# Attention with two wide fp32 parts instead of three bf16 parts, heads stacked in partition halves, and value matmuls carried into the next step

## The reference

```python
x = x + attn(layernorm(x))
# attn: 16 heads of 16 columns, each batch 1024 positions
q, k, v = x @ Wq, x @ Wk, x @ Wv
k_eff1 = w[0] * k1 + w[1] * k2          # w = softmax(quadrant_weights)
k_eff2 = w[2] * k1 + w[3] * k2
attn = softmax((q1 @ k_eff1.T + q2 @ k_eff2.T) * scale)
out = (attn @ v) @ Wo
```

## Time and profile before

| | us |
|---|---|
| median of 3 runs (2004.94 to 2010.0) | 2007.19 |
| the profiled execution | 2008.85 |
| its span | 2007.1 |

### The profile page before, as it was taken

The page is one execution under the profiler, slowest core; times in us unless marked ns, Lnnn a source line. Parts: engine busy times, 40 slices in busy tenths (PEclk is TensorE's granted clock), DMA queues, the critical chain, the costliest instruction groups (busy, mean ns, idle before and its releaser), DMA issues. The chain is left out here.

```text
span 2007.1 us, 38130 instructions
## 1 busy us (share of the span) xinstructions
PE 1746.5 (87%) x10689; PEld 1076.5 (54%) x10690; DVE 1293.4 (64%) x2730; ACT 1016.1 (51%) x2046; POOL 458.4 (23%) x597
## 2 busy tenths in 40 slices
PE   6949999999999999998869986999978549999990
PEld 5802333233233233222758875989876249988880
DVE  7759888788788788871458868555546662222224
ACT  4614777667677677777235432344322225554442
POOL 4636000000000000000101224322122155555550
PEclk9957999999999999999879997999988759999995
DMA  4562221122221122200010001131311922222117
GB/s 152 162 149 32 33 33 33 35 33 33 35 33 33 35 33 33 33 1 1 0 12 1 0 11 44 44 84 42 85 43 51 339 91 66 65 65 65 63 63 259
DMA packets 119479, 121.80 MB, mean 61 GB/s; under 512 B 20692, under 2 KB 97512, under 8 KB 119208
## 3 DMA queue, kind: packets, MB, share of 16 engines
q1 hardware_dynamic: 106568, 94.35, 19.9%
q0 software_dynamic: 7584, 20.72, 3.2%
q10 hardware_dynamic: 5184, 4.98, 0.7%
HBM read 88.04 MB, written 31.59 MB: 60 GB/s over the span
## 5 line engine op out<-in xcount | busy, mean ns | idle before, releaser
L1873 DVE TENSOR_REDUCE mx<-ps 128x1 f32<-128x512 f32 x1024 | 634.9, 682 | 104.5 <-PE ps L2020 104.2
L1947 ACT ACTIVATE PR<-ps 128x512 f32<-128x512 f32 x1024 | 533.9, 607 | 189.5 <-PE ps L2081 186.1
L2020 PE MATMUL ps<-KQ 96*128 96x512 bf16 x1024 | 408.7, 405 | 34.2 <-PEq L210 25.3
L2081 PE MATMUL ps<-KQ 99*128 99x512 bf16 x1024 | 391.8, 389 | 18.5 <-issue 9.8
L2020 PEld LDWEIGHTS ps<-KQ 96*128 96x128 bf16 x1024 | 99.5, 99 | 360.0 <-DVE mx L1873 270.1
L2046 PE MATMUL ps<-PR,VO 128*32 128x512 f32 x2048 | 270.3, 606 | 0.0
L2081 PEld LDWEIGHTS ps<-KQ 99*128 99x128 bf16 x1024 | 99.7, 98 | 143.7 <-ACT PR L1947 59.2
L1968 POOL COPY VO<-V 128x512 f32 (+1 forms) x16 | 9.8, 615 | 719.8 <-PE ps L2046 719.6
L1746 PEld LDWEIGHTS ps<-e_xinT,e_w 128*128 128x128 f32 x1264 | 156.6, 195 | 5.8 <-issue 1.9
L1746 PE MATMUL ps<-e_xinT,e_w 128*128 128x128 f32 x1264 | 157.5, 279 | 1.1 <-ACT e_xinT L1678 1.1
L1736 PE MATMUL ps<-eW,e_hiddenT 128*128 x632 | 154.9, 388 | 3.1 <-issue 1.1
(11 more groups left out here) (289 smaller groups left out, 2354.0 us busy)
## 6 DMA issues: line engine op xcount, KB each, us to landing
KQ<-qk_parts SPq DMA_DIRECT2D x192, 128.0 KB, 4.7
TB<-toeplitz_lines SPq DMA_DIRECT2D x32, 512.0 KB, 5.9
qk_parts<-parts SPq DMA_DIRECT2D x8, 1536.0 KB, 6.8
eW<-in_L_ffn_W SPq DMA_DIRECT2D x16, 512.0 KB, 6.3
eW<-in_L_ffn_W SPq DMA_DIRECT2D x8, 1024.0 KB, 12.0
e_got<-expert_outputs SPq DMA_DIRECT2D x16, 512.0 KB, 9.7
X<-in_L_attn_x SPq DMA_DIRECT2D x8, 512.0 KB, 4.7
expert_inputs<-e_xn SPq DMA_DIRECT2D x8, 512.0 KB, 3.2
```

The source lines that it names most:

```text
L1873: nc.vector.reduce_max(mx[:, k, h, q:q + 1], ps[:, bank(r, ("max", t))], AX).then_inc(red_done, 1)
L1947: nc.scalar.activation(PR[:, kt % 2, h, qc * BANK:(qc + 1) * BANK], ps[:, st_bank(r, s)], ACT.Exp).then_inc(exp_done, 1)
L2020: nc.tensor.matmul(ps[:, bank(r, ("max", t))], KQ[r][0:KROWS, 1, h, q * P:(q + 1) * P], KQ[r][0:KROWS, 0, h, k * BANK:(k + 1) * BANK], sta ...
L2081: nc.tensor.matmul(ps[:, st_bank(r, s)], KQ[r][0:AROWS, 0, h, kt * P:(kt + 1) * P], KQ[r][0:AROWS, 1, h, qc * BANK:(qc + 1) * BANK], start ...
```

## The change

The two sides `q` and `k` are split into two fp32 parts (the kind that TensorE multiplies in one pass, `F32R`) instead of three bf16 ones, and three pairs of parts are stacked instead of six: 48 rows, 50 with the maxima's two parts. Two heads of a unit lie in partitions 0 to 63, two in 64 to 127 (`HALF`, `HR`). The third split and its copy on ScalarE and GpSimd go; parts are stored as fp32. `load_qk` issues 12 DMAs as before, each for two heads; the rows of maxima take four DMAs instead of three.

The first pass writes the two halves of a row of scores to two neighbouring banks (two pairs of banks in place of three single ones), and one reduction over 1024 elements replaces two over 512 and gives the maximum already negated. `negate` has two operations. `EARLY` still says 12 and `LATE` 4, now counted in rounds of two matmuls.

The blocks go through all key tiles for the first half of the queries, then for the second: 16 steps of four blocks (one per head), one value group per step, into a single bank. A step's value group is issued after the second block of the next step, and the last one of a unit in the first step of the next unit. The output is copied by ScalarE in two halves of 512 (`keep_heads`), in the second step of the next half. `VO` has three buffers. After every block comes one maxima matmul of the next units.

```diff
-PARTS = 3
-PAIR_Q = [0, 0, 1, 0, 2, 1]
-PAIR_K = [0, 1, 0, 2, 0, 1]
+PARTS = 2
+PAIR_Q = [0, 1, 0]
+PAIR_K = [0, 0, 1]
 KROWS = len(PAIR_Q) * HD
 AROWS = KROWS + PARTS
+HALF = P // 2
+HR = HG // 2
...
-                KQ = [sbuf(st, f"KQ{r}", [P, 2, HG, SEQ], BF16) for r in range(2)]
+                KQ = [sbuf(st, f"KQ{r}", [P, 2, HR, SEQ], F32R) for r in range(2)]
...
                     for side, pairs in ((1, PAIR_Q), (0, PAIR_K)):
                         for j, part in enumerate(pairs):
-                            src = pqk.rearrange("s a k p t -> s a (k p) t").rearrange("s a (g h c) t -> s a g c h t", h=HG, c=HD)
-                            sp.dma_start(KQ[r][j * HD:(j + 1) * HD, side],
-                                         src[1 - side, part, ds(g, 1), :, :, ds(SEQ * b, SEQ)].rearrange("g c h t -> (g c) h t")).then_inc(kq_loaded[r], 16)
+                            for y in range(2):
+                                row = HALF * y + HD * j
+                                sp.dma_start(KQ[r][row:row + HD, side].bitcast(F32),
+                                             src[1 - side, part, ds(g, 1), :, HR * y:HR * (y + 1), ds(SEQ * b, SEQ)].rearrange("g c h t -> (g c) h t")).then_inc(kq_loaded[r], 16)
...
-                                for m in range(2 * DK):
-                                    pool.wait_ge(mid_ready, 2 * DK * c + m + 1)
-                                    nc.gpsimd.tensor_tensor(part(h, m, 2), rest[:, m], part(h, m, 1), op=ALU.subtract).then_inc(lo_ready, 1)
...
-                                    dve.wait_ge(lo_ready, 2 * DK * c + m + 1)
-                                    nc.vector.tensor_tensor(rest[:, m], ps[:, 2 + m], part(h, m, 0), op=ALU.subtract).then_inc(rest_ready, 1)
+                                    nc.vector.tensor_tensor(part(h, m, 1), ps[:, 2 + m], part(h, m, 0).bitcast(F32), op=ALU.subtract).then_inc(lo_ready, 1)
...
-                                for m in range(2 * DK):
-                                    act.wait_ge(rest_ready, 2 * DK * c + m + 1)
-                                    nc.scalar.copy(part(h, m, 1), rest[:, m]).then_inc(mid_ready, 1)
...
-    VO = sbuf(stack, "VO", [P, KT, HG, 2 * HD])
...
+    VO = sbuf(stack, "VO", [P, RING, KT, HG, 2 * HD])
...
-    SLOTS = 3
-    MAX_BANK, ST_BANK, OT_BANK = 0, SLOTS, 2 * SLOTS
+    SLOTS, PAIRS = 3, 2
+    MAX_BANK, ST_BANK, OT_BANK = 0, 2 * PAIRS, 2 * PAIRS + SLOTS
...
-    BLOCKS, MAXES, NM = KT * HG * QC, HG * QT * QC, 5
-    order = [(h, q, k) for h in range(HG) for q in range(QT) for k in range(QC)]
-    LOADS = 2 * len(PAIR_Q)
+    STEPS = QC * KT
+    BLOCKS, MAXES, NM = STEPS * HG, HG * QT, 2
+    ROWS = 2 * PARTS
+    order = [(HR * y + x, q) for q in range(QT) for x in range(HR) for y in (1, 0)]
+    LOADS = 4 * len(PAIR_Q)
     EARLY = 12
-    TURN = EARLY + 8
-    LATE = 5
+    TURN = EARLY + 5
+    LATE = 4
...
+            nc.vector.memset(nmp[:], 0.0).then_inc(ready, 1)
...
-                nc.vector.reduce_max(mx[:, k, h, q:q + 1], ps[:, bank(r, ("max", t))], AX).then_inc(red_done, 1)
-            def negate(u):
+                nc.vector.tensor_reduce(mx[:, r, h * QT + q:h * QT + q + 1], ps[:, b:b + 2].rearrange("p a n -> p (a n)"), AX, ALU.max, negate=True).then_inc(red_done, 1)
...
+            def keep_heads(u, qc):
+                act.wait_ge(pv_done, STEPS * u + KT * (qc + 1))
+                if not is0(u):
+                    act.wait_ge(ot_tr, u)
+                nc.scalar.copy(OT[:, qc * BANK:(qc + 1) * BANK], ps[:, OT_BANK]).then_inc(ot_kept, 1)
...
                 for s in range(BLOCKS):
-                    kt, h, qc = s // (HG * QC), s // QC % HG, s % QC
+                    step, h = s // HG, s % HG
+                    kt = step % KT
                     act.wait_ge(st_done, BLOCKS * u + s + 1)
-                    if h == 0 and qc == 0 and not (is0(u) and kt < 2):
-                        act.wait_ge(pv_done, KT * u + kt - 1)
-                    nc.scalar.activation(PR[:, kt % 2, h, qc * BANK:(qc + 1) * BANK], ps[:, st_bank(r, s)], ACT.Exp).then_inc(exp_done, 1)
-                    if nxt is not None and s == (BLOCKS - 8 if at(2) is not None else BLOCKS - 1):
-                        keep_rows(nxt[0], (nxt[2] + 1) % RING)
-                act.wait_ge(pv_done, KT * u + KT)
-                if not is0(u):
-                    act.wait_ge(ot_tr, 2 * u)
-                nc.scalar.copy(OT[:], ps[:, OT_BANK:OT_BANK + 2].rearrange("p a n -> p (a n)")).then_inc(ot_kept, 1)
+                    if h == 0 and not (is0(u) and step < 2):
+                        act.wait_ge(pv_done, STEPS * u + step - 1)
+                    nc.scalar.activation(PR[:, kt % 2, h], ps[:, st_bank(r, s)], ACT.Exp).then_inc(exp_done, 1)
+                    if kt == 1 and h == 0:
+                        if step > KT:
+                            keep_heads(u, 0)
+                        elif not is0(u):
+                            keep_heads(u - 1, 1)
+                    if nxt is not None and s == QC * (MAXES - EARLY + LATE) - 2:
+                        keep_rows(nxt[0])
             unit_loop(act, unit)
+            keep_heads(UNITS - 1, 1)
...
-            def weigh(u, kt, qc):
-                if qc == 0:
-                    pe.wait_ge(exp_done, BLOCKS * u + HG * QC * (kt + 1))
-                if kt == 0 and qc == 0:
+            def weigh(u, r, step):
+                kt = step % KT
+                pe.wait_ge(exp_done, BLOCKS * u + HG * (step + 1))
+                if step == 0:
                     pe.wait_ge(vo_ready, u + 1)
-                    if not is0(u):
-                        pe.wait_ge(ot_kept, u)
+                if kt == 0 and not (is0(u) and step == 0):
+                    pe.wait_ge(ot_kept, 2 * u + step // KT)
                 for h in range(HG):
-                    last = nc.tensor.matmul(ps[2 * HD * h:2 * HD * (h + 1), OT_BANK + qc], VO[:, kt, h], PR[:, kt % 2, h, qc * BANK:(qc + 1) * BANK],
+                    last = nc.tensor.matmul(ps[2 * HD * h:2 * HD * (h + 1), OT_BANK], VO[:, r, kt, h], PR[:, kt % 2, h],
                                             start=(kt == 0), stop=(kt == KT - 1))
-                if qc == QC - 1:
-                    last.then_inc(pv_done, 1)
+                last.then_inc(pv_done, 1)
...
                 for s in range(BLOCKS):
-                    kt, h, qc = s // (HG * QC), s // QC % HG, s % QC
+                    step, h = s // HG, s % HG
+                    kt, qc = step % KT, step // KT
                     if not (is0(u) and s < SLOTS):
                         pe.wait_ge(exp_done, BLOCKS * u + s - SLOTS + 1)
-                    nc.tensor.matmul(ps[:, st_bank(r, s)], KQ[r][0:AROWS, 0, h, kt * P:(kt + 1) * P],
-                                     KQ[r][0:AROWS, 1, h, qc * BANK:(qc + 1) * BANK], start=True, stop=True).then_inc(st_done, 1)
-                    if kt > 0 and h in (1, 3) and qc == 1:
-                        weigh(u, kt - 1, h // 2)
-                    while done < (s + 1) * len(beside) // BLOCKS:
-                        what, given = beside[done]
-                        what(*given)
-                        done += 1
-                for qc in range(QC):
-                    weigh(u, KT - 1, qc)
+                    nc.tensor.matmul(ps[:, st_bank(r, s)], KQ[r][half(h, AROWS), 0, h % HR, kt * P:(kt + 1) * P],
+                                     KQ[r][half(h, AROWS), 1, h % HR, qc * BANK:(qc + 1) * BANK], start=True, stop=True).then_inc(st_done, 1)
+                    t, k = divmod(s, QC)
+                    if t + EARLY < MAXES:
+                        if nxt is not None:
+                            first_pass(*nxt, t + EARLY, k)
+                    else:
+                        if after is not None:
+                            first_pass(*after, t + EARLY - MAXES, k)
+                    if s == QC * (TURN - EARLY) - 1 and not is0(u):
+                        turn_heads(u - 1)
+                    if s == QC * (MAXES - EARLY + LATE) - 1 and nxt is not None:
+                        turn_max(nxt[0])
+                    if h == HR - 1:
+                        if step > 0:
+                            weigh(u, r, step - 1)
+                        elif not is0(u):
+                            weigh(u - 1, (r + RING - 1) % RING, STEPS - 1)
```

More of the change, by code:

```diff
@@ L1906, in _ @@
                 reduce(0, 0, t)
-            negate(0)
+            negate(0, 0)
             for t in range(EARLY):
@@ L1986, in unit @@
                 (u, n, r), nxt, after = at(0), at(1), at(2)
-                sp.wait_ge(row_loaded[r], 16 * PARTS * (n + 1))
-                if after is not None and not is0(u):
+                sp.wait_ge(row_loaded[r], 16 * ROWS * (n + 1))
+                if is0(u):
+                    sp.wait_ge(ones_ready, 2)
+                elif after is not None:
                     sp.wait_ge(st_done, BLOCKS * u)
@@ L2023, in turn_max, with first_pass @@
-            def turn_max(u, r):
```

(24 more changed lines are left out.)

140 lines of the change are left out of this document (56 added, 84 removed).

## The result

The changed kernel takes 2029.8 us (median, 2024.8 to 2040.7) against 2007.9 of the kernel before on the same chip: 1.011 times as long, 95% interval 1.0088 to 1.0131. It is slower, clear of the noise, where 1972.5 was forecast, and the time lies outside the range of 1948 to 2008. The profiled execution has a span of 2030.4 us against 2007.1: +23.3, where the sum said -36.1.

A forecast was written before the change was run, and what follows sets the result against it. TensorE was taken as the bound. Stage start -1, before the loop +6.1, unit 0 -5, 14 units at -2.9 each and last unit +4.4 sum to -36.1: 2008.85 to 1972.8, kept as 1972.5 us; range 1948 to 2008.

The forecast's parts named there:

- The halves work at once, a pair costs 0.22: Loop: block and maxima matmul on different partition halves overlap, 0.22 us a pair; 0.44 if they don't.
- The rival "turns": Loop: the halves don't overlap, step 2.85 to 2.93 us, total 2036 to 2053, middle 2043; chance 0.14.
- Value group 1.00, ScalarE 0.49 per exponential, VectorE not the bound, idle 0.6 and 0.3 a step: Loop: operation times in us; VectorE needs 38.9 a unit, below 41.1; ScalarE idles 0.6, VectorE 0.3 per step.
- Step 2.57: Loop: chain of exponential, value group, block 3, its exponential 0.43 later, and exponential 4 makes a step 2.57 us.
- The partial rival: Loop: serial weight loads or a dearer value group, step 2.67, unit 47.1 or 47.2, about 1993 us; chance 0.14.
- Extras 4.4: Each loop unit: output copies 1.96, output transposes and wait 1.5, transposed maxima 0.9, together 4.4 us beyond 16 steps.
- Last unit +4.4: Last unit, without maxima: step from 2.40 to 2.57 (+2.7), two copies +2.0, boundary -0.3: 4.4 us longer.
- The rival "the clock": Loop: clock at half for a third of it, step at least 3.9 us, +120, about 2090; chance 0.03.
- Before the loop +6.1: Before the first block: 12 early rounds of full 1024, the last waiting for ten reductions; first block 6.1 us later.
- Unit 0 -5, stage start -1, rest 0: First unit 5 us shorter at 44; projection with loads and stores 1 us shorter; remaining program unchanged.

The follow-up runs named there:

- the two experiments on them: Changed kernel with last-unit dummy matmuls and copies moved before the third exponential: 1985.8 us; changed kernel with value group after the fourth block: 1986.6 us.
- The experiment: Changed kernel plus an unread matmul of the maxima's shape after each block left without a maxima matmul, mainly in the last unit: 2015.9 us.
- the pair of executions above: Changed kernel with value group after the fourth block, without and with the last unit's dummy matmuls: 1986.6 and 1977.5 us.

## Why the prediction was wrong, point by point

- *The halves work at once, a pair costs 0.22*: right. Pairs start together, and 0.24 from the next when TensorE runs on. The rival "turns" was built and gave the step it named, 2.83 for 2.85.
- *Value group 1.00, ScalarE 0.49 per exponential, VectorE not the bound, idle 0.6 and 0.3 a step*: right, within 0.02.
- *Step 2.57*: the term that failed is the 0.43 from a block to its exponential. It was read in the last unit of before, on a bf16 block, whose weight load of 0.10 stands behind the group too; the fp32 load there takes 0.18, and the way to the exponential 0.53. The row that says so was on the table: 195 against 99 ns in the earlier trace rows. I had used it for TensorE's sum, where it is hidden behind other matmuls, and not on the chain, where nothing hides it. 16 x 0.10 x 14 units = 22 us. The partial rival named this size, 2.67 and a unit of 47.1, for another reason.
- *Extras 4.4*: measured 4.8, of which the copies are 1.9 as counted. The copies' mechanism and size were right, and of the two experiments on them one took 1.3 of a unit away and the other 1.9; the rest of the extras was not measured term by term.
- *Last unit +4.4*: the main failure. I had weighed the clock for the loop alone, and for the last unit taken from the earlier trace rows that it stays at 1.00. But that row is of matmuls with 99 rows. In the changed kernel the loop has both halves at work and the last unit only one, and its granted clock is 0.61 in the mean from the last mark on. The experiment puts this at 22.7 us in that stretch, 24.7 in the span, 14 by the medians. The rival "the clock" had half clock at the wrong place, in the loop, at a chance of 0.03; and its argument, the share of time at work, doesn't tell the loop (2.0 of 2.67 us, 0.98) from the last unit (1.97 of 2.67, 0.61).
- *Before the loop +6.1*: measured +13.9. Three terms were too small: a reduction at half clock takes 1.27 and not 1.18 (44 of them, 4.0); three places where two rounds share a pair of banks (3 x 1.15 = 3.4), which the sum didn't have; and 2.4 instead of 2.0 for the memsets. They make the difference, 7.8. Where unit 0's bank pairs go by turns, two of the three places are gone and the first block comes 3.1 earlier than with 8 early rounds alone.
- *Unit 0 -5, stage start -1, rest 0*: the start gave 2.8 more and the rest 1.7 more. Of the +32.3 by which the first and last unit together missed, 22.7 is the clock and 1.6 the step of the last unit; the other 8 are not taken apart. Unit 0 is at half clock for its first 9.7 us (to 192.0), before for 3.5; at the 6.2 us that 19.8 us at half clock cost in the pair of executions above, that is an estimated 2. Of the loop's 24, a unit of 47.5 instead of 45.6 makes 14 x 1.9 = 27, 22 of it the step; the units at the turn of the hardware loop, which the sum did not look at, give some of it back.
- *Three sums*: the unit's terms add up to 45.5, not 45.6. In the partial rival, loads at 0.19 make a step of 8 x 0.19 + 1.09 = 2.61 and a unit of 46.2, not 47.2. And 1.06 and 1.2 over two slots are 1.13 a reduction, not 1.18, further from the measured 1.27. None changes which terms failed.

In one sentence: the change did what the forecast said it does in the loop, at 16.7 of the 40.6 us of gain, and the gain that was left was smaller than what the ends lost.

## What to carry to other kernels

Take the latency of a link in a chain from a row with the same type, and look at whether its weight load can hide: behind a value group or a wait it starts with its matmul in every row shown here. When a change halves the rows that a matmul uses, ask in every stretch, the last one too, whether the other half still has work, since the granted clock may follow it, as it did here in the last unit; a few matmuls that do nothing can then be cheaper than idle rows. Before moving the work itself, move who waits for a buffer: two blocks later was worth 2 us a unit.

## What the runs showed of the hardware that I had not expected

- With the two row halves by turns the mean granted clock of 14 units was 0.89, TensorE busy for 736 of 785 us; with both at once 0.98, busy for 599 of 682 and for 671 of 769.
- In the last unit, with one row half at work, the clock fell to 0.50 without a pause of TensorE above 0.45 us, 13 us behind the last mark in one order of the value group and 44 us behind it in the other.
- Added matmuls, 84 of them, shortened the profiled span by 24.7 us and the median by 14.
- An fp32 matmul whose weight load starts with it, behind a value group or a wait, lasts 0.49 to 0.50 instead of 0.39, and 0.47 with 96 weight columns instead of 128.
- Two executions of the same code before unit 1 differed by 6 us through the moment at which the clock came back.
